# Joint pass of a graph and attention layer: edge lists loaded earlier, and column maxima of the next edge set turned ahead of the sums of this one

## What is computed

```python
xn = layernorm(x)
x = x + gnn(xn, edges) + mix(xn)      # gnn: two graph attention layers; mix: kernelised attention
x = x + ffn(layernorm(x))             # 8 experts, two of them chosen for each node

# one graph attention layer, per head:
e = leaky_relu(al_s[src] + al_d[dst], 0.2)
m = segment_max(e, dst)
ex = exp(e - m[dst])
out = segment_sum(h[src] * ex / segment_sum(ex, dst)[dst], dst)

# mix, key side: keys and values from xn @ w_qkv.T, then
data_dash = (d ** -0.25 * k) @ proj.T
k_prime = exp(data_dash - diag - max(data_dash)) + eps
context = k_prime.T @ v
```

## Time and profile before

| | us |
|---|---|
| median of 3 timed runs | 4491.92 (4491.79 to 4496.94) |
| the profiled execution | 4493.03 |
| its span in the profile | 4491.0 |
| TensorE busy | 3867.0 (86%) |
| VectorE busy | 2145.9 (48%) |
| GpSimd busy | 1355.0 (30%) |
| ScalarE busy | 1169.2 (26%) |

### The profile page before, as it was taken

One profiled execution on the slowest core, in us unless ns is written; L12 is line 12 of the kernel. 1 busy time (PEld: TensorE's weight loads), 2 busy tenths in 40 slices (PEclk: granted clock), 3 DMA queues, 4 the chain that ended last, 5 costly groups with the idle time before them and its releaser, 6 DMA issues. The chain is left out here.

```text
span 4491.0 us, 67390 instructions
## 1 busy us (share of the span) xinstructions
PE 3867.0 (86%) x23483; PEld 3123.4 (70%) x23484; DVE 2145.9 (48%) x4835; ACT 1169.2 (26%) x2391; POOL 1355.0 (30%) x1368
## 2 busy tenths in 40 slices
PE   6774988988988849999699958988988669999998
PEld 5773666666666638888699955555555369999997
DVE  6853555555555634444322215555555345445444
ACT  1222333323333323333211102222222122222222
POOL 1123555555555500000000025666666201111110
PEclk8887999999999969999899978999999779999999
DMA  5765666666666433332555647888888420000000
GB/s 204 259 236 197 209 203 205 208 208 206 202 207 213 149 136 133 138 140 112 133 78 79 81 154 250 295 292 295 299 295 284 160 80 29 21 21 28 21 21 14
DMA packets 239565, 729.54 MB, mean 162 GB/s; under 512 B 75503, under 2 KB 80650, under 8 KB 230995
## 3 DMA queue, kind: packets, MB, share of 16 engines
q0 software_dynamic: 88000, 374.95, 26.3%
q1 hardware_dynamic: 151315, 351.47, 25.4%
HBM read 642.07 MB, written 145.41 MB: 175 GB/s over the span
## 5 line engine op out<-in xcount | busy, mean ns | idle before, releaser
L873 POOL DMA_INDIRECT k_rows<-tab,k_pick x576 | 593.1, 1030 | 498.3 <-PE k_num L1293 350.2
L1995 POOL DMA_INDIRECT m_rows<-tab,m_e x500 | 491.6, 983 | 324.3 <-PE m_out L2288 178.9
L1293 PE MATMUL k_num<-k_rows,k_wt 128*64 128x384 f32 (+1 forms) x2400 | 453.1, 530 | 32.2 <-ACT k_wt L960 32.1
L1293 PEld LDWEIGHTS k_num<-k_rows,k_wt 128*64 128x64 f32 x2400 | 176.0, 148 | 260.4 <-issue 215.2
L133 PE MATMUL g_prod<-g_w_hi,g_h_h 128*128 128x384 f32 x800 | 270.4, 338 | 1.5 <-DVE g_h_l L1594 1.5
L135 PE MATMUL g_prod<-g_w_hi,g_h_l 128*128 128x384 f32 x800 | 268.2, 335 | 0.0
L134 PE MATMUL g_prod<-g_w_lo,g_h_h 128*128 128x384 f32 x800 | 268.0, 335 | 0.0
L133 PE MATMUL f_prod<-f_w_hi,f_a_h 128*128 128x512 f32 x600 | 244.1, 407 | 0.0
L1455 DVE TENSOR_TENSOR f_a_l<-f_turn,f_a_h 128x384 fp32r<-128x384 f32 x200 | 110.6, 553 | 262.5 <-ACT f_a_h L1431 262.0
L135 PE MATMUL f_prod<-f_w_hi,f_a_l 128*128 128x512 f32 x600 | 235.5, 392 | 0.0
L134 PE MATMUL f_prod<-f_w_lo,f_a_h 128*128 128x512 f32 x600 | 233.9, 390 | 0.0
(11 more groups left out here) (292 smaller groups left out, 8935.2 us busy)
## 6 DMA issues: line engine op xcount, KB each, us to landing
agg<-k_outb SPq DMA_DIRECT2D x100, 384.0 KB
f_a_in<-agg SPq DMA_DIRECT2D x100, 384.0 KB
h<-f_e SPq DMA_DIRECT2D x25, 1024.0 KB, 4.1
g_h<-h SPq DMA_DIRECT2D x25, 1024.0 KB, 12.1
tab<-q_xn SPq DMA_DIRECT2D x25, 388.5 KB, 6.0
tab<-g_row SPq DMA_DIRECT2D x25, 385.5 KB, 4.6
m_own<-tab SPq DMA_DIRECT2D x25, 385.5 KB
q_x<-in_x SPq DMA_DIRECT2D x25, 384.0 KB, 6.5
```

The source lines that it names most:

```text
L873: pool.indirect_dma_start(rows[:, place(u, n), :], None, dram["tab1"], at, bounds_check=bound, oob_is_err=False).then_inc(rows_in[i], 16)
L1293: mm = pe.matmul(num[i][64 * g:64 * g + 64, 0:n], wt[:, 2 * c + g, :], rows[:, place(u, 2 * c + g), a:a + n], start=(c == 0), stop=(c == 2 ...
L1995: pool.indirect_dma_start(rows[:, place(h, c) + k, :], None, tab, bass.IndirectOffsetOnAxis(ap=e[h % 4][:, 0, k * SLOTS + c:k * SLOTS + c ...
```

## The change

Six things are changed, all in the merged variant:
- Edge lists. `load_edges(1)` is issued at the start, behind the first `load_xt` and ahead of three small constant loads. In the loop `load_edges(t + 2)` is issued in quarter 3 in place of `load_edges(t + 1)` in quarter 1. The buffers stay two.
- `z` and `wt` become one pair of buffers `wt[0]`, `wt[1]`: the logits of set `u` are formed in `wt[u % 2]`, and the shift and the exponential work in place.
- TensorE: a quarter begins with `edge_spread(u)`, and `edge_turn` of set `u + 1` (`next_set`) stands ahead of `edge_sums(u)`.
- VectorE: `shift(u)` comes directly behind the denominator, `column_max(u + 1)` behind `maxima` (in quarter 3 behind `k_low`), and in quarter 3 the penalties and `logits(u + 1)` come ahead of `k_low` and `scale_values`. `logits(0)` moves to quarter 3 of `t = 0`.
- ScalarE: `weights(u)` comes directly behind `result(u - 1)`, ahead of the copies.
- `logits(u)` waits for the sums of set `u - 2` in place of the shift of `u - 1`, since the buffer is theirs; the shift no longer waits for the sums of `u - 1`.

```diff
--- before.py
+++ after.py
@@ -764,7 +764,7 @@
             rel, far = s.sb2("rel", [P, 24]), s.sb("far", [P, 24])
             pick = [s.sb(f"pick{b}", [P, 24], I32) for b in range(3)]
             pen, ald = s.sb("pen", [P, 24, SG]), s.sb2("ald", [P, 4 * P])
-            z, wt, zmax = s.sb("z", [P, SLOT, GH * SG]), s.sb("wt", [P, SLOT, GH * SG]), s.sb("zmax", [P, P])
+            wt, zmax = s.sb2("wt", [P, SLOT, GH * SG]), s.sb("zmax", [P, P])
             mcol, dg, den, rden = s.sb("mcol", [P, 1]), s.sb("dg", [P, P]), s.sb("den", [P, 1]), s.sb("rden", [P, 1])
             outb = s.sb("outb", [P, D])
             zbank, num = s.bank("zbank"), [s.bank(f"num{i}") for i in range(2)]
@@ -784,6 +784,11 @@
         def set_of(t, quarter):
 
             u = 4 * (t - 1) + quarter
+            return u if merged and 0 <= u < SETS else None
+
+        def next_set(t, quarter):
+
+            u = 4 * (t - 1) + quarter + 1
             return u if merged and 0 <= u < SETS else None
 
         @blk.sync
@@ -821,6 +826,8 @@
                 if merged:
                     load_edges(0)
                 load_xt(0)
+                if merged:
+                    load_edges(1)
                 sp.dma_start(pad[:, :], io["pad_rows"]).then_inc(c_in, 16)
                 if merged:
                     sp.dma_start(offs[:, :], io["group_offsets"].partition_broadcast(P)).then_inc(c_in, 16)
@@ -831,8 +838,8 @@
                             load_xt(t + 1)
                         if merged and quarter == 0 and t < NT:
                             load_ald(t)
-                        if merged and quarter == 1 and t + 1 < NT:
-                            load_edges(t + 1)
+                        if merged and quarter == 3 and t + 2 < NT:
+                            load_edges(t + 2)
                         u = set_of(t, quarter)
                         if u is not None and u >= 1:
                             store(u - 1)
@@ -956,7 +963,7 @@
 
                 def weights(u):
                     act.wait_ge(shift_done, u + 1)
-                    wf = wt[:, :, :].rearrange("p c n -> p (c n)")
+                    wf = wt[u % 2][:, :, :].rearrange("p c n -> p (c n)")
                     act.activation(wf, wf, ACT.Exp).then_inc(wt_done, 1)
 
                 if merged:
@@ -966,6 +973,8 @@
                         u = set_of(t, quarter)
                         if u is not None and u >= 1:
                             result(u - 1)
+                        if u is not None:
+                            weights(u)
                         if t < NT and quarter < 2:
                             k_copy(t, quarter)
                         if merged and quarter == 2 and t + 1 < NT:
@@ -974,8 +983,6 @@
                             v_copy(t, quarter - 2)
                         if quarter == 3 and 1 <= t <= NT:
                             scales(t - 1)
-                        if u is not None:
-                            weights(u)
                         if quarter < 3 and 1 <= t <= NT:
                             exps(t - 1, 2 * quarter)
                         if quarter == 3 and t < NT:
@@ -1108,8 +1115,9 @@
                     t, i = u // 4, u % 4
                     dve.wait_ge(rows_in[i], 16 * SLOT * (u // 4 + 1))
                     dve.wait_ge(pen_done, t + 1)
-                    if u:
-                        dve.wait_ge(shift_done, u)
+                    if u >= 2:
+                        dve.wait_ge(num_full, u - 1)
+                    z = wt[u % 2]
                     head = min(SLOT, RING - place(u, 0))
                     for a, n in ((0, head), (head, SLOT - head)):
                         if n:
@@ -1144,9 +1152,8 @@
 
                 def shift(u):
                     dve.wait_ge(mrow_full, u + 1)
-                    if u:
-                        dve.wait_ge(num_full, u)
-                    dve.tensor_tensor(wt[:, :, :].rearrange("p (c g) n -> p c (g n)", g=2), z[:, :, :].rearrange("p (c g) n -> p c (g n)", g=2),
+                    z = wt[u % 2]
+                    dve.tensor_tensor(z[:, :, :].rearrange("p (c g) n -> p c (g n)", g=2), z[:, :, :].rearrange("p (c g) n -> p c (g n)", g=2),
                                       zbank[:, P:2 * P].unsqueeze(1).to_broadcast([P, 3, P]), ALU.subtract).then_inc(shift_done, 1)
 
                 def denominator(u):
@@ -1166,39 +1173,36 @@
                     penalty(0)
                 for t in range(NT + 2):
                     for quarter in range(4):
-                        u = set_of(t, quarter)
+                        u, nx = set_of(t, quarter), next_set(t, quarter)
                         if u is not None:
                             if u >= 1:
                                 denominator(u - 1)
-                            else:
-                                logits(0)
-                            column_max(u)
+                            shift(u)
                         if t >= 2 and quarter < 2:
                             rescale(t - 2, 2 * quarter)
                         if quarter == 3 and 1 <= t <= NT:
                             running_max(t - 1)
-                        if u is not None:
-                            shift(u)
                         if t >= 2 and quarter < 2:
                             rescale(t - 2, 2 * quarter + 1)
                         if merged and quarter == 2 and t + 1 < NT:
                             indices(t + 1)
-                        if u is not None and u + 1 < SETS and not (quarter == 3):
-                            logits(u + 1)
+                        if quarter == 3 and merged and 0 <= t < NT and t:
+                            penalty(t)
+                        if nx is not None:
+                            logits(nx)
                         if quarter < 3 and 1 <= t <= NT:
                             maxima(t - 1, 2 * quarter)
+                        if quarter == 3 and t < NT:
+                            k_low(t, 0)
+                            k_low(t, 1)
+                        if nx is not None:
+                            column_max(nx)
                         if quarter == 2 and 1 <= t <= NT:
                             row_max(t - 1)
                         if quarter == 3:
                             if 1 <= t <= NT:
                                 scale_values(t - 1)
-                            if merged and 1 <= t < NT:
-                                penalty(t)
-                            if u is not None and u + 1 < SETS:
-                                logits(u + 1)
                             if t < NT:
-                                k_low(t, 0)
-                                k_low(t, 1)
                                 diag(t)
                 if merged:
                     denominator(SETS - 1)
@@ -1290,7 +1294,7 @@
                     for c in range(3):
                         for i, (a, n) in enumerate(HALF):
                             for g in range(2):
-                                mm = pe.matmul(num[i][64 * g:64 * g + 64, 0:n], wt[:, 2 * c + g, :], rows[:, place(u, 2 * c + g), a:a + n],
+                                mm = pe.matmul(num[i][64 * g:64 * g + 64, 0:n], wt[u % 2][:, 2 * c + g, :], rows[:, place(u, 2 * c + g), a:a + n],
                                                start=(c == 0), stop=(c == 2), tile_position=(0, 64 * g), skip_group_check=True)
                     mm.then_inc(num_full, 1)
 
@@ -1299,15 +1303,13 @@
                     index_turns(0)
                 for t in range(NT + 2):
                     for quarter in range(4):
-                        u = set_of(t, quarter)
+                        u, w = set_of(t, quarter), next_set(t, quarter)
                         if u is not None:
-                            edge_turn(u)
+                            edge_spread(u)
                         if t >= 2 and quarter < 2:
                             contexts(t - 2, 2 * quarter)
                         if t < NT:
                             product(t, quarter)
-                        if u is not None:
-                            edge_spread(u)
                         if t >= 2 and quarter < 2:
                             contexts(t - 2, 2 * quarter + 1)
                         if merged and quarter == 2 and t + 1 < NT:
@@ -1319,6 +1321,8 @@
                         if quarter == 3 and t < NT:
                             k_turns(t, 0)
                             k_turns(t, 1)
+                        if w is not None:
+                            edge_turn(w)
                         if u is not None:
                             edge_sums(u)
                 pe.wait_ge(vsum_done, NT)
```

## The result

| | before | after |
|---|---|---|
| median, us | 4491.85 (4488.94 to 4496.94) | 4674.45 (4670.82 to 4681.35) |
| ratio | 1 | 1.0407 [1.0389, 1.0425] |
| span of the profiled execution | 4491.0 | 4674.4 |
| joint pass, from the MEMSET of its ones to the start of its last matmul | 351.1 to 1592.5 = 1241.4 | 351.9 to 1775.5 = 1423.6 |
| period of a tile in the pass | 47.8 | 54.5 |

A forecast was written before the change was run, and what follows sets the result against it. TensorE was taken to bound the joint pass. Waits of 236.2 less 173.5 removed (+62.7), clock +172.2 and start +5 made +240 on 4493.0, less 1.1: 4732 us, 5.3% slower, range 4565 to 4800 for 8 in 10.

The forecast's parts named there:

- The bound: Joint pass: TensorE bounds it, busy 1011 of 1133 us at clock 0.93; its idle time and clock decide.
- What is removed: TensorE's waits at L1273 (90.2) and the sums (29.8), plus slow stretches behind L1273 (53.5): 173.5 us go.
- The moved store: Quarter 3's store behind the list issues delays ScalarE in quarter 0: nothing under cover, up to 4 us per tile without.
- The added waits: Turn of the next set's maxima waits for VectorE's zmax in every quarter: 236.2 us in total.
- Rival 3: Turn hardly waits in quarters 0 and 1, decided at the rescale ahead of the logits: about 4466 us; 5%.
- The clock: TensorE's clock slows behind each added wait: +172.2 us, bounds nothing to 226.
- The term of 69 x 1.65: Slow clock behind the three kinds of turn wait of 2.04 to 2.48 us, quarters 0 to 2: 113.9 us.
- The clock forecast for the pass: New profile's granted clock in the joint pass clearly below 0.93, near 0.8.
- Start and end: load_edges(1) ahead of small loads delays the second tile: +5 us, between 0 and 20; last tile 0, within 8.
- The clock that holds: Rival 1: waits as forecast, clock never halved or only behind the 3.56 us wait: 4560 to 4618 us; 17%.
- Rival 2: Slow stretches outlast one set of sums: 4786 us; 14% for more than 4770.
- rival 4: Edge numbers still late because SyncE is now behind in quarter 0: 143.7 us come back, 4876; 2%.

The follow-up runs named there:

- the last experiment: Kernel before with edge lists in four portions, and in quarter 3 the shift ahead of the running maximum and weights ahead of scales: 4351.5 us, ratio 0.9684.
- the order alone: Changed kernel with load_edges back at its places of before (one tile ahead, quarter 1): 4866.4 us, ratio 1.0557.
- the portions under the same cover: Changed kernel with its own order on all engines, edge lists issued in four portions behind the stores: 4680.1 us, ratio 1.0416.
- the logits first: Changed kernel with VectorE's next logits directly behind the shift in every quarter: ratio 1.0100 with lists in one piece, 0.9904 in four portions.
- the order of before: Kernel before with only the edge lists moved two tiles ahead: ratio 1.0169 in one block in quarter 3, 0.9852 in four portions.

## Why the prediction was right in its direction and wrong in one size

- **The bound.** Right. TensorE's idle time and clock in the pass are the whole difference, 128.0 + 54.2 = 182.2.
- **What is removed.** Right as a size. The wait of 90.2 at L1273 and most of the 29.8 at the sums went, and so did the slow stretches behind L1273. Their 53.5 us, worked out as 22 x 2.43, are borne out by the 52.9 us between the kernel before and the last experiment, which has two slow sums in place of 24. The total of that experiment is 138 us below before and not 173.5; the difference is 26.8 us more at the turn (31.6 against 4.8) and the 7.4 that stay at the sums. What the removal was put down to was wrong in one point: the order alone, with the lists where they were, leaves 5.8 us at this place from 450 on (49.5 before on such a chip). In the changed kernel the wait is gone mostly because the tile is longer.
- **The moved store.** Right in its cost here and in its condition, too low in the price without the cover. In the changed kernel the lists end at 1005.49 and the store goes at 1005.54, behind all 18 transfers as the step says; ScalarE's next result waits, but for something else:

```profile
1004.13 1.36 SPq L814 DMA_DIRECT2D k_e<-in_node_ints  x2
1005.54 0.45 SPq L824 DMA_DIRECT2D agg<-k_outb  x1
...
1010.86 1.05 ACT L908 ACTIVATE k_outb<-k_num,k_rden 128x384 f32<-128x384 f32 x2 [7.88 <-DVE k_rden L1167]
```

  The denominator is later than the store, since it stands behind sums that themselves stood behind a wait. With the portions under the same cover the time stayed the same (1.0416 against 1.0407); without the cover the store costs 96 us of pass with the logits first, about the forecast "up to 4 us per tile", and 143.5 in the order of before, 6.2 per tile.
- **The added waits.** Right, quarter by quarter: 2.17, 2.10, 2.54 and 3.27 us in the tile shown, 2.04, 2.04, 2.48 and 3.56 forecast, in sum 253.9 against 236.2. The last was put too long by 0.29; the key turns, taken with the 0.91 us of the earlier trace rows, now last 1.14 and cover 0.23 more of VectorE's chain. The first wait of the pass, 7.02 us (4.78 before), is in the 253.9 and was not in the 236.2. Rival 3's place was the right one in quarters 0 and 1: where the logits go ahead of the rescale, that wait is gone.
- **The clock, the step that failed.** Forecast +172.2 for 93 slow stretches, less 53.5 for the 22 that go: net +119. Measured: net +54 (106.6 less 52.9, or 54.2 in the pass by itself). The price of one was not far off: 106.6 us on 51 slow sums is 2.1, between the 1.65 and the 2.43 of the forecast. The count was: 51, not 93. The term of 69 x 1.65 is the one that was mis-sized most: of the 46 sums in quarters 0 and 1 that it priced as slow, at most 7 were. A price was taken for each wait from the row of its like, 1.92 us and a clock of 0.59, and added up. The runs show that it doesn't add. The same 2.1 us wait stands ahead of full speed sums with four waits to a tile and ahead of slow ones with two, and the busy time of all sums is 499.5, 491.4 and 503.2 us with four, two and two. Rows like the earlier trace rows say that a wait of 2 us can be followed by 1.2 GHz, not that each one is.
- **The clock forecast for the pass.** "Near 0.8" was too low even by the forecast's own terms. Before, 0.07 of 1133 us is 79 lost; 79 - 53.5 + 172.2 = 198 of the 1373 forecast gives 0.86. It is 0.93 from 450 to 1400 in both kernels, since a longer stretch divides the loss. A tile was forecast at 57 to 58 us and takes 54.5.
- **Start and end.** +5 forecast. The second tile's first turn is at 412.97, 2.2 later than before. The first gather came at 399.63, as worked out (399.3), but less of it arrived at TensorE.
- **The rivals.** The clock that holds (4560 to 4618) fell. The rule of the Trainium skill that stood behind it, page TensorE: Matmul & The Clock Gate, section "Loop structure matters more than you think", says that VectorE's copy out of PSUM between two output tiles "doesn't break PE warmth"; there the next matmuls "follow immediately", a condition that the prediction left out. In these traces TensorE has to wait, and the rule doesn't hold for that: 3.27 us for VectorE, then 24 sums in 5.79 us instead of 4.10. The same page's section "A second HAM failure mode", that short idles between groups of matmuls cost throughput, agrees with it. Rival 2 fell too: behind the slow sums the matmuls of the product take 0.33 to 0.34 us each, as in the tile's other quarters. The lists were in time, so rival 4 fell. 4674 is inside the range and 58 below the forecast: 65 too much at the clock, and 7 too little at TensorE's idle time (128.0 measured; 116.2 of waits and 5 at the start forecast). The two errors have opposite signs, so a small part of the nearness is luck.

**What stays open.** Which of several waits in a tile is followed by the slow clock: the counts above show that it depends on more than the wait, the rest of the tile among it, and not by what rule. On the 4613 us chips part of the waits is put down to nothing that the profile shows (87.7 us at the turn, in 30 pieces, in the changed kernel), and why those chips are slower in the second pass stays open; in it VectorE waits 208.8 us in 41 pieces for something that the profile only calls remote, and the trace of 4491 us has no such row.

## What to carry to other kernels

Before a step that waits is moved ahead of work that used to cover it, find what it waits for and ask what stands ahead of that on its own engine; here the producer's four operations stood behind an idle time of 3.87 us, and on the 4613 us chips a ratio of 1.049 fell to 1.027 when the turn alone was put back, and to 1.010 when instead its producer was moved ahead. A block of 18 DMA issues on a queue that also carries stores holds whoever waits for a store by up to 20 us, and moving the block moves the stall, unless other waits cover it: divide it instead. A cost of zero holds under its cover only, so carry the condition along when parts of a change are tried alone. And give the clock's share a range, from no slow stretch to one for each wait, rather than a price for every wait: how many of the waits are followed by one wasn't told by their length.

## What was not expected of the hardware

- The clock doesn't follow single waits. With two waits of 2.1 us in a tile, the sums of 44 of 50 sets behind them ran slow; with two more of 2.5 and 3.3 us in the tile, 7 of 50 behind the same two did, and 44 of 50 behind the longer ones.
- TensorE at a granted clock of 1.00 from 409 to 1400 came with shorter waits, not with fewer instructions: 956 us busy in 991, with no wait of TensorE over 1.1 us from 425 on.
- Two of three chips ran the kernel before in 4613 us in place of 4490, the second joint pass in 951 us in place of 803, but the first in 1213.6 in place of 1241.4. A difference of 3% between chips goes both ways within one kernel; only ratios on one chip can be read.
